# Two graph layers in one kernel: the similarities' other half by block transposes and DRAM, not by TensorE

## The reference

```
h   = relu(layernorm(x))
z_l = h W_lang^T ;  z_g = h W_grav^T ;  v = h W_V^T
A_l = relu(cosine(z_l, z_l)) off the diagonal
A_g = exp(-|z_g - z_g'|^2 / (2 sigma^2)) off the diagonal
K   = w_l * rownorm(A_l * adj) + (1 - w_l) * rownorm(A_g * adj)
x   = x + (K v) W_O^T
x   = x + (adj * adj)^T relu(layernorm(x)) + bias
```

## Time and profile before

| what | value |
|---|---|
| median of three runs | 1273.1 us (1272.77 to 1273.65) |
| the profiled execution | 1273.19 us, its span 1271.3 us |
| TensorE busy | 1242.1 us, 98% |
| VectorE busy | 1059.6 us, 83% |
| ScalarE busy | 695.0 us, 55% |
| GpSimd busy | 573.6 us, 45% |
| mean granted clock of TensorE | 0.996 |

### The profile page before, as it was taken

How to read it: one execution, slowest core, us unless ns; L and a number is a source line. 1 busy time by engine, 2 the same in 40 slices (tenths; PEclk the granted TensorE clock), 3 DMA queues, 4 the chain that set the end, 5 groups by cost and what they waited for, 6 DMA issues and landing times.

```text
span 1271.3 us, 22572 instructions
## 1 busy us (share of the span) xinstructions
PE 1242.1 (98%) x6324; PEld 1039.8 (82%) x6324; DVE 1059.6 (83%) x1826; ACT 695.0 (55%) x1324; POOL 573.6 (45%) x964
## 2 busy tenths in 40 slices
PE   7899999999999999999999999999999999999996
PEld 6778888888888888888888888888888888888884
DVE  5578888988888988888988888898888898888878
ACT  5446554566555456555456655456655546655534
POOL 1015544345554445553434554434554444555334
PEclk9999999999999999999999999999999999999998
DMA  6223333433424442423442433443342444242201
GB/s 242 34 56 94 77 72 99 107 97 85 95 54 101 105 105 79 105 58 91 99 107 83 99 75 73 99 107 94 88 94 55 99 107 103 79 107 56 60 34 66
DMA packets 308894, 112.55 MB, mean 89 GB/s; under 512 B 269840, under 2 KB 269968, under 8 KB 308880
## 3 DMA queue, kind: packets, MB, share of 16 engines
q1 hardware_dynamic: 177360, 95.78, 27.7%
q10 hardware_dynamic: 131520, 16.60, 7.9%
HBM read 46.20 MB, written 33.62 MB: 63 GB/s over the span
## 4 chain that ended last, share of the span: by engine, by line
PE 94%; DVE 3%; issue 1%; ACT 1%; DMA 1%; POOL 0%; SPq 0%; DVEq 0%; ACTq 0%
PE ring L862 77%; PE p_ps L862 14%; PE p_ps L935 2%; PE kt_ps L875 1%; DMA h2f<-in_L_gnn_W_grav 1%; DVE x_out L686 0%; ACT h L379 0%; DVE bn L635 0%; DVE x_ring L629 0%; DVE y_lo L782 0%; DVE hT_lo L555 0%; ACT h2f L469 0%; DVE Lw_lo L797 0%; DVE bn L566 0%; SPq L236 0%
## 5 line engine op out<-in xcount | busy, mean ns | idle before, releaser
L301 POOL TENSOR_TENSOR x_out<-x_ring,bias_sb 128x512 f32<-128x512 f32 x128 | 162.8, 1294 | 499.9 <-DVE bn L635 499.9
L406 ACT ACTIVATE y_hi<-ring 128x512 fp32r<-128x512 f32 x256 | 148.6, 592 | 207.4 <-PE ring L862 204.3
L862 PE MATMUL ring<-hT_hi,Lw_hi 128*128 128x512 f32 x640 | 255.7, 399 | 3.7 <-DVE hT_lo L574 2.1
L862 PE MATMUL ring<-hT_hi,Lw_lo 128*128 128x512 f32 x640 | 250.6, 392 | 0.0
L862 PE MATMUL ring<-hT_lo,Lw_hi 128*128 128x512 f32 x640 | 250.2, 391 | 0.0
L862 PE MATMUL ring<-MT_hi,hT_hi 128*128 128x512 f32 x512 | 202.4, 395 | 0.0
L555 DVE TENSOR_TENSOR v_lo<-ring,v_hi 128x512 fp32r<-128x512 f32 x128 | 88.5, 692 | 136.1 <-ACT v_hi L442 136.1
L862 PE MATMUL ring<-MT_lo,hT_hi 128*128 128x512 f32 x512 | 199.8, 390 | 0.0
L862 PE MATMUL ring<-MT_hi,hT_lo 128*128 128x512 f32 x512 | 199.4, 390 | 0.0
L308 POOL TENSOR_TENSOR h_lo<-h2f,h_hi 128x512 fp32r<-128x512 f32 x124 | 158.1, 1296 | 85.0 <-ACT h_hi L476 85.0
L555 DVE TENSOR_TENSOR y_lo<-ring,y_hi 128x512 fp32r<-128x512 f32 x256 | 169.2, 681 | 29.9 <-ACT y_hi L406 29.8
(11 more groups left out here) (160 smaller groups left out, 2539.0 us busy)
## 6 DMA issues: line engine op xcount, KB each, us to landing
x_ring<-in_x SPq DMA_DIRECT2D x32, 1024.0 KB, 5.6
out<-x_out SPq DMA_DIRECT2D x128, 256.0 KB, 2.2
h_turned<-h SPq DMA_DIRECT2D x248, 64.0 KB, 2.1
h_turned<-h ACTq DMA_DIRECT2D x248, 64.0 KB, 2.1
rn_cols<-rn_dram SPq DMA_DIRECT2D x31, 256.0 KB, 3.8
x_ring<-in_L_gnn_W_lang SPq DMA_DIRECT2D x4, 256.0 KB, 5.5
h2f<-in_L_gnn_W_grav SPq DMA_DIRECT2D x1, 1024.0 KB, 8.9
chain<-in_L_gnn_W_O SPq DMA_DIRECT2D x1, 1024.0 KB, 12.9
```

Source lines behind the costliest of these rows:

```text
L301: pool.tensor_tensor(x_out[:, b], x_rows(g, b), bias_sb[:, :], ALU.add).then_inc(x2b_ready, 1)
L406: act.activation(y[0][:, a, :, l], bank(n).rearrange("p (b m) -> p b m", b=GB), ACT.Copy)\
L862: mm = pe.matmul(out, lhsT, rhs, start=(k == 0), stop=(k == len(terms) - 1))
```

## The change

The transposes of P leave TensorE in all iterations but the last, which keeps the old way (`sum_s_last`). VectorE transposes each half of `P_sb` in 32x32 blocks into the memory of `diag` (`turn_p`), the language half before the first `v_lo`, the gravity half after it, once it has been shifted. SyncE stores both halves, 512 KB, to DRAM, waits for that, and loads them back with four DMAs of 128 KB that exchange the blocks, into the first two rows of `h`. VectorE sums the language half alone (`sum_s`), GpSimd the gravity half (`sum_g`, after `norm1` in the next iteration).

With that, the steps behind move into the next iteration: `sum_s`, `similarities` and `mask_l` after the first `y_lo`, `mask_g` after the second, `row_factors` after the third, `combine` after the fourth as before; `exponentials` after ScalarE's second `y_hi`; `turn_blocks` after the fifth and sixth `y_lo`. `normalize` waits for both sums, since they read memory of `h`.

```diff
+            def turn_p(g):
+                sp.wait_ge(p_blocks, 2 * g + 2)
+                sp.dma_start(p_dram, P_blocks.rearrange("p j b l q -> p j (b l q)")).then_inc(p_stored, 16)
+                sp.wait_ge(p_stored, 16 * g + 16)
+                for j in range(NQ):
+                    sp.dma_start(P_turned[j * Q:(j + 1) * Q], p_dram[:, j].rearrange("(i r) e -> r i e", r=Q))\
+                      .then_inc(p_turned, 16)
...
                     spread_norms(i)
+                    turn_p(i)
                 store_out(i - 1, first_use(i) + PER - GB)
...
+            def sum_g(g):
+                pool.wait_ge(p_turned, 16 * NQ * (g + 1))
+                turned_g = P_turned.rearrange("p i (b l q) -> p b l i q", b=GB, l=2)[:, :, 1]
+                pool.tensor_tensor(A[:, :, 1].rearrange("p b (i q) -> p b i q", q=Q), turned_g,
+                                   P_sb[:, :, 1].rearrange("p b (i q) -> p b i q", q=Q), ALU.add).then_inc(sg_ready, 1)
...
                     norm1(i + 1)
                 if before:
+                    sum_g(i - 1)
...
+                        if before and n == 2:
+                            exponentials(i - 1)
                         if after and 3 <= n < 5:
                             normalize(i + 1, (n - 3) * GB // 2)
...
                         if before and n == 1:
+                            sum_s(i - 1)
+                            similarities(i - 1)
+                            mask_l(i - 1)
+                        if before and n == 2:
                             mask_g(i - 1)
-                        if before and n == 2:
+                        if before and n == 3:
                             row_factors(i - 1)
-                        if after and n == 4:
-                            turn_blocks(i + 1, 0)
-                            turn_blocks(i + 1, 1)
                         if before and n == 4:
                             combine(i - 1)
                         if after and n == 5:
+                            turn_blocks(i + 1, 0)
+                            turn_blocks(i + 1, 1)
+                        if after and n == 6:
                             turn_blocks(i + 1, 2)
                             turn_blocks(i + 1, 3)
...
+            def turn_p(g, l):
+                if l == 0:
+                    dve.wait_ge(sq_ready, 3 * g + 2)
+                    wait_for(dve, p_stored, 16 * g)
+                else:
+                    dve.wait_ge(p_shifted, g + 1)
+                dve.transpose(P_blocks[:, :, :, l].rearrange("p j b q -> p b j q"),
+                              P_sb[:, :, l].rearrange("p b (j q) -> p b j q", q=Q)).then_inc(p_blocks, 1)
...
             def sum_s(g):
-                dve.wait_ge(pt_done, g + 1)
+                dve.wait_ge(p_turned, 16 * NQ * (g + 1))
+                turned_l = P_turned.rearrange("p i (b l q) -> p b l i q", b=GB, l=2)[:, :, 0]
+                dve.tensor_tensor(A[:, :, 0].rearrange("p b (i q) -> p b i q", q=Q), turned_l,
+                                  P_sb[:, :, 0].rearrange("p b (i q) -> p b i q", q=Q), ALU.add).then_inc(s_ready, 1)
...
-                    if b == (2 if after else 0):
+                    if b == 0 and not after:
                         pe.wait_ge(p_shifted, i + 1)
                         for k in range(2 * GB):
                             mm = pe.transpose(p_ps[:, k // 2, k % 2], P_sb[:, k // 2, k % 2], ident[:, :])
                         mm.then_inc(pt_done, 1)
```

More of the change, by code:

```diff
@@ L103, in gnn_pair @@
         h_turned = sb("h_turned", [P, GB, C, P])
+        P_blocks = diag.rearrange("p b l m -> p (b l m)").rearrange("p (j b l q) -> p j b l q", j=NQ, b=GB, l=2)
+        P_turned = h[:, 0:2].rearrange("p b d -> p (b d)").rearrange("p (i e) -> p i e", i=NQ)
         h_blocks = h[:, :, :].rearrange("p b (c j q) -> p j (b c) q", c=C, j=NQ)
@@ L115, in gnn_pair @@
         woT_parts = [w[:, :, :] for w in h2]
+        p_dram = nc.dram_tensor("p_dram", [P, NQ, GB * 2 * Q], F32).ap()
         rn_dram = nc.dram_tensor("rn_dram", [P, GB], F32).ap()
@@ L155, in gnn_pair @@
         p_shifted = sem("p_shifted")
-        s_ready = sem("s_ready")
+        s_ready, sg_ready = sem("s_ready"), sem("sg_ready")
         sq_ready = sem("sq_ready")
@@ L172, in gnn_pair @@
         rn_step = sem("rn_step")
+        p_blocks, p_stored, p_turned = sem("p_blocks"), sem("p_stored"), sem("p_turned")
         def passes(hi_lo_lhs, hi_lo_rhs):
@@ L247, in _ @@
             spread_norms(0)
+            turn_p(0)
             sp.wait_ge(w_split, 3 * C)
@@ L377, in normalize @@
                         act.wait_ge(turned, TURN * (g - 1))
+                        act.wait_ge(s_ready, g - 1)
+                        act.wait_ge(sg_ready, g - 1)
                 for b in range(b0, b0 + GB // 2):
@@ L426, in iteration @@
                     act.wait_ge(s_ready, i)
-                    act.wait_ge(diag_ready, 2 * i)
+                    act.wait_ge(sg_ready, i)
                 for half in range(2):
@@ L439, in iteration @@
                     if not after and b == 1:
-                        exponentials(i)
+                        exponentials(i, last=True)
                     act.wait_ge(v_done, GB * i + b + 1)
@@ L458, in iteration @@
                         h2_copy(i - 1, 3)
-                if after:
-                    exponentials(i)
             def h2_full(g, b, last=False):
@@ L482, in shift, with exponentials @@
                 e.then_inc(p_shifted, 1)
-            def exponentials(g):
-                act.wait_ge(s_ready, g + 1)
+            def exponentials(g, last=False):
+                act.wait_ge(s_ready if last else sg_ready, g + 1)
                 act.activation(A[:, :, 1], A[:, :, 1], ACT.Exp, scale=inv_sig2).then_inc(exp_done, 1)
@@ L725, in iteration @@
                 squared_norms(i)
+                turn_p(i, 0)
                 for b in range(GB):
@@ L731, in iteration @@
                     turned_lo(i + 1, b)
-                    if b == 2:
-                        sum_s(i)
+                    if b == 0:
+                        turn_p(i, 1)
                 if before:
@@ L736, in iteration, with sum_s_last @@
                         output(i - 1, b, n + b)
-                similarities(i)
-                mask_l(i)
-            def sum_s(g):
-                dve.wait_ge(pt_done, g + 1)
+            def turn_p(g, l):
[6 more added lines that the diff above has]
+                              P_sb[:, :, l].rearrange("p b (j q) -> p b j q", q=Q)).then_inc(p_blocks, 1)
+            def sum_s(g):
+                dve.wait_ge(p_turned, 16 * NQ * (g + 1))
+                turned_l = P_turned.rearrange("p i (b l q) -> p b l i q", b=GB, l=2)[:, :, 0]
+                dve.tensor_tensor(A[:, :, 0].rearrange("p b (i q) -> p b i q", q=Q), turned_l,
+                                  P_sb[:, :, 0].rearrange("p b (i q) -> p b i q", q=Q), ALU.add).then_inc(s_ready, 1)
+            def sum_s_last(g):
+                dve.wait_ge(pt_done, 1)
                 dve.tensor_tensor(A, p_ps[:, :, :, :], P_sb, ALU.add).then_inc(s_ready, 1)
@@ L765, in last_chain @@
                 v_lo(0)
-                sum_s(i)
+                sum_s_last(i)
                 similarities(i, last=True)
@@ L936, in iteration @@
                         mm.then_inc(pt_done, 1)
-                        if not after:
-                            transposes_rn(i)
+                        transposes_rn(i)
                 if before:
```

## The result

| | before | after |
|---|---|---|
| median | 1273.38 us (4 runs, 1272.77 to 1273.82) | 1355.78 us (4 runs, 1355.35 to 1356.41) |
| ratio | | 1.0648, 95% interval 1.0629 to 1.0666 |
| span of the profiled execution | 1271.3 us | 1353.6 us |
| TensorE busy | 98% | 92% |

The account below looks back on a forecast made before the run. TensorE bounds the kernel, with VectorE's handovers equally tight; the changed loop runs through GpSimd, ScalarE and VectorE. 1273.2 + 80.0 (29 periods at +2.76) + 1.7 (iteration 1) + 1.1 (iteration 31) = 1356 us; range 1310 to 1385.

Parts of the forecast that it names:

- The bound and where it was tight: Whole kernel: TensorE bounds it, two VectorE handovers before K's transposes and k_v equally tight; 1356 us, period 40.52, +2.76.
- the start: Iteration 1: +2.86 at its k_v, less 0.87 for iteration 0 and a little for GpSimd, together +1.7 us.
- What the removal is worth: Iteration's end: of TensorE's 0.87 us per iteration only 0.1 counts, bounds 0.1 to 0.87.
- The 27 us: TensorE's transposes of P: 31 x 0.87 us, the gain if TensorE alone set the time.
- `turned_lo` getting in ahead of `h2_lo`: Iteration's end, alternative order: the last layer1, needing h2_lo, would be next, some 0.5 us gained.
- The tight half: First y to k_v: sums delay the chain; K transposed at 12.5 not 11.08, k_v at 17.37 not 14.51 us.
- The two engines blocking each other: VectorE and GpSimd on SBUF: exclusive lock, loser blocks a whole instruction; sum_g 3.05 to 4.3, similarities to 5.4.
- the second rival: VectorE's similarities and mask_l go ahead of sum_g, or loads late: period +3.2 to +3.8, 1369 to 1387 us; chance 0.22.
- The first rival: No blocking: sums run side by side, loop over ScalarE, period 39.2, +1.46, 1317 us; chance 0.2.
- The DMAs: Store and loads through DRAM: store 4.5, last load 2.6 us, in at 608.5, hidden with 1.3 us to spare.
- my signs of being wrong: Chain: sum_g ending before 3.5, kt_lo before 14.5, or VectorE's wait for the loads starting the chain.
- this order stays: Iteration's end: h2_lo, turned_lo, then four outputs keep their order, so only 0.1 of 0.87 us counts.

Follow-up runs that it names:

- e1: Kernel before without TensorE's eight transposes of P in iterations 0 to 30, nothing in their place: 1272.78 us, ratio 0.9995.
- e3: Changed kernel with the block transpose of the fourth graph's input moved behind kt_lo: 1333.82 us, ratio 1.0468 to the kernel before.
- e2: Changed kernel with both sums on VectorE, gravity first, and GpSimd taking no part: 1344.55 us, ratio 1.0553 to the kernel before.
- f3: Changed kernel with GpSimd's sum doubled by one more instruction of the same inputs and size: 1385.51 us, ratio 1.0876 to the kernel before.
- e4: Changed kernel without the store to DRAM and four loads, sums reading the unexchanged blocks in place: 1350.71 us, ratio 1.0602 to the kernel before.
- e7: Changed kernel with h2_lo of the third graph on VectorE instead of GpSimd: 1344.19 us, ratio 1.0550 to the kernel before.
- e5: Kernel before, P still transposed on TensorE and one VectorE sum, but later steps in the change's new places: 1340.94 us, ratio 1.0521.
- e9: Changed kernel with both sums and one h2_lo on VectorE, block transposes moved, P stored earlier, similarities and mask_l fused: 1259.07 us, ratio 0.9873 to the kernel before.
- f1: Kernel before with the third graph's h2_lo on VectorE behind the old sum, and similarities and mask_l fused: 1290.79 us, ratio 1.0130.
- f2: As f1, but without TensorE's eight transposes of P and nothing in their place: 1289.35 us, ratio 1.0125 to the kernel before.
- f4: As f1, but with VectorE's h2_lo ahead of the old sum of 1024 columns: 1274.25 us, ratio 1.0002 to the kernel before.

## Why the prediction was right

- **The bound and where it was tight: right.** 1356 was predicted, 1355.78 measured. From the first K transposed to the 31st are (1304.08 - 91.48) / 30 = 40.42 us, against 37.75 before: +2.67 in place of +2.76 per period, 80 us of the 82.3. The rest is the start, +1.4, predicted +1.7, and 0.8 behind the 31st. That the time came out to 0.2 us is luck: 30 periods at +2.67 stand where 29 at +2.76 were reckoned, and some of the +2.67 is the waits for the loads, which the forecast had at nothing.
- **What the removal is worth: 0.1 us said, 0.0 found.** e1 shows it on the kernel before, where nothing else was changed. The 27 us that the chain of waits alone suggests would have been wrong by all of it, since a second chain of the same length, over ScalarE, GpSimd and VectorE, ran beside TensorE's. The 0.5 us that the prediction had for `turned_lo` getting in ahead of `h2_lo` was too much: by the rows above 0.3 is all that the last `layer1` leaves.
- **The tight half: right in place, and in size to 0.3 us.** K transposed at 12.44 (12.5) and `k_v` at 17.28 (17.37) in the iteration shown, where the loads were late; at 12.2 and 17.05 in most, so the way itself was reckoned some 0.3 us too long. `similarities` is 1.99 us long (over 2). ScalarE, `combine` and the way to `kt_lo` came as worked out, and e3 confirms the last.
- **The two engines blocking each other: right.** `sum_g` went between `sum_s` and `similarities`, as the forecast had it and the second rival had not. e2 and f3, one without it and one with it twice, give 11 and 30 us. In the kernel after `similarities` is 1.98 to 2.01 us long in all but the first and the last iteration. In the first GpSimd began 0.04 us ahead of VectorE, and there `sum_s` is the long one, 1.80 us, and `similarities` 1.09. The first rival, no blocking, is out by these rows. Its price of 1317 us stays untested: e2, with no GpSimd in it, is at 1345, but has 0.6 us more per iteration on VectorE.
- **The DMAs: this term was off.** I had the loads in at 1.1 us after the first `y`, with 1.3 to spare; in the iteration shown they landed at 2.5, and `sum_s` waited 0.17 us. The last load was taken at 2.6 and took 2.8, the store at 4.5 and took 4.36 here, with a median of 4.8 over the run; but the store was issued 0.96 us after the blocks, since SyncE stood in its wait for the norms, and the loads' issues were 0.43 and not 0.33 us apart. I had named the queue, and not what its wait costs. A wait for the loads was one of my signs of being wrong: it is there in 7 of 31 iterations, and it is not what made the kernel slower. It stayed small, 5 us by e4, because in the other iterations the loads were in before VectorE and GpSimd's `norm1` were ready for them; e7 shows that it takes some of other gains.
- **`turned_lo`:** that it is 0.83 us longer than alone (1.52 against 0.69) was in the forecast only as "this order stays"; the blocking that I had priced elsewhere is its reason.

## What to carry to other kernels

When an engine is busy 98% and another hands over to it with 0.3 us to spare, relieving the first can give nothing until the second has room: count the loop through the other engines before counting the instruction that goes. Work moved past the point at which its result was just in time costs its whole delay (e5: `k_v` 2.14 us later after the first `y`, and the period as much longer), and engines that are half idle don't make up for it if their queue is in the wrong order. Before GpSimd gets a share of VectorE's work, look which of VectorE's instructions with two SBUF inputs stands next: give GpSimd the time in which VectorE reads PSUM (e9: GpSimd's product ran beside the four outputs, which kept their 2.47 us).

## What the runs showed of the hardware

- Where both engines want SBUF, GpSimd and VectorE alternate in these runs, and the one that waits gets the next turn: in f3 `sum_s`, GpSimd's copy, `similarities`, GpSimd's sum, `mask_l` follow each other, although VectorE's three stand directly behind one another in its queue. 0.02 us decided in f1 who waited: 1.82 in place of 0.69 us.
- GpSimd's 128x512 product with one operand read at a step of four elements took 1.57 us (e9; 1.55 to 1.56 in f1, f2 and f4), beside 1.30 us for its contiguous sums and differences. That the step is the reason was not tested.
- The same store of 512 KB to DRAM landed 4.8 us after its issue behind the spreading of the norms (256 KB read by all partitions from one row) and 2.8 us when issued ahead of it; the spreading took 4.2 and 4.0 us. All of these are medians. In the page's part 6 of the kernel after, and of e9:

```profile
p_dram<-chain SPq DMA_DIRECT2D x31, 512.0 KB, 4.8
```
```profile
p_dram<-chain SPq DMA_DIRECT2D x31, 512.0 KB, 2.8
```
